# Filling the slots table in five parts from SP, spreading the first modulation by a product, and k's sum as a column of kv

## The chip, the cores and the metric
The kernel is one program on one core of a Trainium2 chip. The metric is the device time in microseconds of one execution, the median of several runs. Five engines work side by side: TensorE (PE; its weight loads are shown apart as PEld), VectorE (DVE), ScalarE (ACT), GpSimd (POOL) and SyncE (SP, which here mostly issues DMAs). They meet only through semaphores.

## The reference
Two transformer layers on x of shape (4, 1024, 128), each with an adaptive-norm modulation computed from a vector c per batch. Cut to what matters here, which is layer 0:

```
mod = (silu(L0_c) @ L0_wmod).reshape(4, 6, 1, -1)      # sa, ca, ga, sb, cb, gb
ga  = (2 * (ga >= 0) - 1) * maximum(abs(ga), 0.25)     # gb likewise
h = layernorm(x) * (1 + ca) + sa
# linear attention, 16 heads of 8, inside L0_attn_ref(h)
q = elu(q) + 1 ; k = elu(k) + 1
kv   = einsum('bhnd,bhne->bhde', k, v)
ksum = sum(k over n)
z    = 1 / (einsum('bhnd,bhd->bhn', q, ksum) + 1e-6)
attn_out = einsum('bhnd,bhde->bhne', q, kv) * z
# projection, residual, layer norm, MLP; x = x + ga * that
# then h = layernorm(x) * (1 + cb) + sb; x = x + gb * mixture(h), top 4 of 16 experts and 2 shared
```

Layer 1 has softmax attention with 16 heads of 64 and a position bias, and a mixture of 8 experts, top 2, with a shared part. Its routed tokens are sorted through a table in DRAM: for every expert there is a region of 4096 rows, and each token row is scattered to its slot.

## The kernel before
The residual x (four batches of 1024 tokens) stays in SBUF as `xs`. The program has five stages: a setup; a loop over the four batches that does all of layer 0 and the first norm of layer 1 (stored to DRAM as `hkeep`); layer 1's attention, a software pipeline over 64 heads, by far the longest; a loop over batches that routes tokens and scatters rows into `slots`; and a loop over 72 tiles of 128 rows of `slots` for the experts.

Each engine has its own instruction stream, in program order. At the end of a stage or a batch every engine calls `end_batch` (drain, count up `batch_ended`, wait for `batch_open`), and SP calls `meet`: it waits until all four others have ended, clears the batch's semaphores and opens the next. So a batch starts when the last of the five is there.

**Setup.** SP issues the loads (lines 327 to 346), waits for the modulation rows computed by PE and VectorE (`mod_one`), stores them to DRAM (`modrows`, line 349), waits until they have landed, and loads them back spread over 128 partitions: `modnext` (line 331: the first two rows, for the batch to come), and for every batch `modwo` and `modd` (lines 356, 357: eight DMAs). Before the first meeting it waits for `next_mod` and `rows_in`. VectorE computes the moments of batch 0's x, finishes the modulation rows (752 to 765), copies constants (768 to 777, `set_done`), treats the transposed modulations (782 to 793), then normalizes batch 0's x (`first_norm`, line 742), applies modnext (line 800), takes the moments again and normalizes a second time. POOL fills constants and one SBUF tile, `spair`, with the mark EMPTY, and raises to the power -0.5 (line 517). ScalarE waits for `set_done` and `pool_set` and writes EMPTY over the whole `slots` table from `spair` with two DMAs (lines 1232, 1233), then goes to the meeting. `filled` counts them; POOL waits for it before layer 1's attention and VectorE in each batch ahead of the first norm of layer 1.

**A layer-0 batch.** PE turns the normalized x (line 1455), projects k and v per tile (1490) and q (1493). VectorE and ScalarE apply elu + 1 to k (817, 820) and to q (822, 824), and VectorE copies v. PE then makes k's column sum (eight products with a column of ones, line 1497), kv (eight products summed in one bank, 1500), the denominators (eight products with 16 columns, 1505) and the numerators (eight products with 128 columns, 1509). VectorE masks ksum by head (828) and kv (830), adds the projection's bias to h (831), adds eps to all denominators at once (834), inverts them (836) and multiplies each half of the numerators by them (841). PE turns the result (1513), VectorE and ScalarE copy a half each (844, 1242), PE projects (1517), and VectorE adds the residual (647). The MLP, the experts and layer 1's first norm follow. In each batch SP issues the whole modulation rows `modb` (line 375) and `modnext` for the next batch, and towards the end stores `hkeep` (381). After the loop SP issues the attention's first eight loads (388 to 399) and then `hT` (408), for which it waits.

## Time and profile before
| | us |
|---|---|
| median of 3 runs (2627.24 to 2631.41) | 2630.47 |
| the profiled execution | 2632.31 |
| its span, first to last instruction | 2630.30 |
| PE, DVE, ACT, POOL busy | 2311.4, 1772.2, 1280.1, 1394.8 |
| setup, until PE's first transposes of batch 0 | 65.4 |
| layer-0 batches 0 and 1 | 122.3 and 119.2 |

PE is busy for 88% of the span, nearly all of it in layer 1's attention. Such a share says little about a stage: the setup and the layer-0 batches are a chain of short steps that pass from engine to engine, so each is read from its timeline and its chain of waits. The granted TensorE clock, 1.00 for 2.4 GHz and 0.50 for 1.2 GHz, was 0.916 on average. DMA moved 83.5 MB in all.

### The profile page before, as it was taken

To read this page: it belongs to the slowest core of one execution; us is meant where nothing else is said; L and a number is where in the kernel's file an instruction comes from. 1 tells how busy PE (TensorE), PEld (TensorE's weight loads), DVE (VectorE), ACT (ScalarE), POOL (GpSimd) and SP (SyncE) were. 2 spreads that over 40 slices of the span, in tenths; PEclk is the share of its full clock that TensorE was granted. 3 is DMA by queue.
4 is the path that set the end of the run, shared out by engine and by line. 5 is a ranking of instruction groups with operands and counts; after the bars stand their busy time and mean duration, and the time that the engine had idled before them with its cause. 6 is when DMAs were issued, how large, how long until landed. Compare 5 with 4: busy or idle time off the path is not lost.

```text
span 2630.3 us, 40209 instructions
## 1 busy us (share of the span) xinstructions
PE 2311.4 (88%) x10587; PEld 1388.2 (53%) x10608; DVE 1772.2 (67%) x4580; ACT 1280.1 (49%) x1705; POOL 1394.8 (53%) x757
## 2 busy tenths in 40 slices
PE   1778786949999999999999999999999976649995
PEld 0645554625555655555555555555555543326664
DVE  3475656557777777877877877877877754544444
ACT  0222121326666666666666666666666641114442
POOL 1120111107777777777777777777677764542321
PEclk6788787859999999999999999999999987869998
DMA  9200000000000000000000000000000011001114
GB/s 357 85 23 0 22 0 22 0 27 14 9 14 13 11 20 13 11 13 12 12 20 12 13 11 12 14 18 12 14 10 11 14 52 75 26 25 45 42 42 121
DMA packets 68566, 83.45 MB, mean 32 GB/s; under 512 B 17732, under 2 KB 55236, under 8 KB 68360
## 3 DMA queue, kind: packets, MB, share of 16 engines
q1 hardware_dynamic: 59784, 56.57, 7.0%
q10 hardware_dynamic: 4384, 17.37, 1.9%
q0 software_dynamic: 4352, 8.99, 1.1%
q8 instruction: 18, 0.29, 0.0%
q14 instruction: 28, 0.23, 0.0%
HBM read 52.33 MB, written 32.66 MB: 32 GB/s over the span
## 4 chain that ended last, share of the span: by engine, by line
PE 81%; DVE 7%; issue 4%; POOL 3%; ACTq 2%; ACT 1%; DMA 1%; SPq 1%; POOLq 0%; DVEq 0%
PE P L1655 17%; PE P L1619 11%; PE P L1640 9%; PE P L1641 9%; PE P L1606 4%; PE P L1828 2%; PE P L1832 2%; PE P L1851 2%; POOL slots L598 2%; PE P L1662 2%; PE P L1673 2%; PE P L1588 2%; PE P L1541 2%; PE P L1555 2%; PE P L1455 2%
## 5 line engine op out<-in xcount | busy, mean ns | idle before, releaser
L1305 ACT ACTIVATE big<-P 128x1024 f32<-128x1024 f32 x512 | 511.9, 1021 | 188.3 <-PE P L1641 84.4
L937 DVE CUSTOM_DVE_ANT_0 big<-P,near 128x512 f32<-128x512 f32 x512 | 348.8, 681 | 231.5 <-PE P L1619 231.2
L1655 PE MATMUL P<-big,V 128*64 128x512 f32 x2048 | 481.4, 602 | 0.0
L560 POOL TENSOR_TENSOR spair<-spair,big 128x1024 f32<-128x1024 f32 x192 | 457.3, 2382 | 13.2
L560 POOL TENSOR_TENSOR opair<-opair,big 128x1024 f32<-128x1024 f32 x192 | 456.9, 2380 | 13.8 <-ACT big L1305 0.7
L1619 PE MATMUL P<-Ka,Qa 96*128 96x512 f32 x1024 | 452.2, 463 | 4.8 <-DVE mhalf L937 3.3
L1640 PE MATMUL P<-Qa,Ka 97*128 97x512 f32 x1024 | 407.8, 398 | 0.5 <-ACT big L1305 0.5
L940 DVE TENSOR_REDUCE mhalf<-P 128x1 f32<-128x512 f32 x512 | 349.2, 682 | 85.9 <-PE P L1619 75.9
L1641 PE MATMUL P<-Qb,Kb 128*128 128x512 f32 x1024 | 406.5, 397 | 0.0
L1619 PEld LDWEIGHTS P<-Ka,Qa 96*128 96x128 f32 x1024 | 186.0, 191 | 224.3 <-issue 118.6
L547 POOL TENSOR_TENSOR big<-big,sinv 128x512 f32<-128x512 f32 x64 | 81.8, 1278 | 377.6 <-DVE sinv L912 377.6
L1655 PEld LDWEIGHTS P<-big,V 128*64 128x64 f32 x2048 | 130.1, 136 | 262.8 <-issue 207.4
L912 DVE RECIPROCAL sinv<-sinv 128x128 f32<-128x128 f32 x256 | 240.9, 943 | 14.7 <-ACT sinv L1291 12.7
L1640 PEld LDWEIGHTS P<-Qa,Ka 97*128 97x128 f32 x1024 | 195.0, 190 | 50.0 <-issue 14.9
L1641 PEld LDWEIGHTS P<-Qb,Kb 128*128 128x128 f32 x1024 | 195.5, 191 | 45.5
L531 POOL TENSOR_TENSOR rstd<-veps,halfneg 128x4 f32<-128x4 f32 x40 | 41.1, 1027 | 240.5 <-DVE veps L635 240.5
L617 POOL DMA_INDIRECT yrows<-xn,tidx x72 | 69.1, 960 | 176.6 <-DVE xn L1189 176.6
L1455 PE MATMUL P<-identf,xn 128*128 128x128 f32 x128 | 36.9, 432 | 136.9 <-DVE xn L641 77.1
L950 DVE TENSOR_TENSOR P<-P,near 128x128 f32<-128x128 f32 x512 | 149.6, 292 | 8.1 <-PE P L1641 6.1
L1606 PE MATMUL P<-hT,wqk 128*128 128x512 f32 x256 | 135.0, 609 | 16.7 <-SPq L410 10.1
L1275 ACT ACTIVATE Qa<-P 64x512 fp32r<-64x512 f32 x128 | 75.7, 591 | 132.7 <-PE P L1641 101.4
L1295 ACT ACTIVATE Qa<-P 1x1024 fp32r<-1x1024 f32 x64 | 64.8, 1012 | 144.7 <-PE P L1624 144.7
(273 smaller groups left out, 3585.8 us busy)
## 6 DMA issues: line engine op xcount, KB each, us to landing
slots<-spair ACTq DMA_DIRECT2D x1, 16896.0 KB, 56.9
Ka<-auxrows SPq DMA_DIRECT2D x66, 128.0 KB, 2.2
big<-in_wex SPq DMA_DIRECT2D x8, 768.0 KB, 9.1
xt<-slots SPq DMA_DIRECT2D x76, 66.0 KB, 1.8
wqk<-in_whead SPq DMA_DIRECT2D x66, 64.0 KB, 1.8
near<-in_aux SPq DMA_DIRECT2D x66, 64.0 KB, 1.8
big<-yrows SPq DMA_DIRECT2D x8, 512.0 KB, 7.2
modb<-modrows SPq DMA_DIRECT2D x4, 768.0 KB, 4.3
```

The costliest lines, as they stand in the source:

```text
L560: pool.tensor_tensor(psum8[s][:, :], psum8[s][:, :], pfull[:, j % RING, :], ALU.add).then_inc(S["p_added"], 1)
L912: dve.reciprocal(sinv[s][:, cols], sinv[s][:, cols]).then_inc(S["s_inv"], 1)
L937: dve.tensor_tensor_reduce(scratch, P[:, 6 + i, :], near[s][:, left:left + HALF], -1.0, 3.0e38, ALU.add, ALU.min, mhalf[:, i, t:t + 1]).th ...
L940: dve.tensor_reduce(mhalf[:, i, t:t + 1], P[:, 6 + i, :], AX.X, ALU.max, negate=True).then_inc(S["max_red"], 1)
L950: dve.tensor_tensor(block, block, near[s][:, ZERO:ZERO + 128], ALU.add).then_inc(S["biased"], 1)
L1305: act.activation(pfull[:, j, :], banks(2 * (j % 2)), ACT.Exp, scale=DH1 ** -0.5).then_inc(S["exp_done"], 1)
L1455: tr = pe.transpose(bank_t(bank, t), src[:, t, :], identf[:, :])
L1606: pe.matmul(P[:, 5, :], wqk[s][:, :], half(hT, i), start=True, stop=True).then_inc(S["qk_mm"], 1)
L1619: pe.matmul(P[:, 6 + i, :], tile(Qa[s][0:MROW, :], t), half(Ka[s][0:MROW, :], i), start=True, stop=True).then_inc(S["max_mm"], 1)
L1640: pe.matmul(P[:, bank + i, :], tile(Ka[s][0:KEXACT, :], j), half(Qa[s][0:KEXACT, :], i), start=True, stop=False)
L1641: mm = pe.matmul(P[:, bank + i, :], tile(Kb[s], j), half(Qb[s], i), start=False, stop=True)
L1655: mm = pe.matmul(P[64 * i:64 * i + 64, 4, :], V1[:, j, s, :], half(pfull[:, j, :], i), start=(j == 0), stop=(j == T - 1))
```

## The change
The `slots` table is no longer filled by ScalarE in the setup. SP issues it in five parts: one in each layer-0 batch (128 partitions x 11 pieces of 768 words, behind the batch's modulation loads) and a tail (128 x 4 pieces of 33 words) ahead of the attention's loads. The source is `later`, which POOL fills instead of `spair`; POOL alone waits for all five, at the end of layer 1's attention.

The first modulation of batch 0 is not loaded from DRAM: PE multiplies a row of ones with the two rows of batch 0 that it needs and so puts them on all 128 partitions of a PSUM bank, and VectorE reads them there. The first load of `modnext` and the waits for it go. In VectorE's setup order the first norm, its modulation and the moments stand ahead of the constants and the transposed modulations.

In the attention of layer 0, v has a column of ones beside its 128 columns (written by POOL in each batch), so kv's product has k's sum as its 129th column. Masked kv and masked ksum lie side by side, and one product of 144 columns per tile gives numerators and denominators. VectorE adds eps, inverts and multiplies once per half. The sum's and the denominators' own products go. Leading blanks are cut below.

```diff
-       "kv_mm", "ks_mm", "kv_masked", "ks_masked", "num_mm", "den_mm", "den_eps", "den_inv", "o0_tok", "o0_turned", "o0_done", "o0_done_a",
+       "kv_mm", "kv_masked", "ks_masked", "num_mm", "v0_ones", "den_eps", "den_inv", "o0_tok", "o0_turned", "o0_done", "o0_done_a",
...
-  "mod_one", "mod_out", "modT_copied", "set_done", "pool_set", "batch_ended", "batch_open", "x_in", "h_kept", "rows_in", "we_in", "passed", "filled", "scattered",
+  "mod_one", "mod_spread", "mod_out", "modT_copied", "set_done", "pool_set", "batch_ended", "batch_open", "x_in", "h_kept", "rows_in", "we_in", "passed", "filled", "scattered",
...
+onerow = sb("onerow", [1, 128])
...
-small = opair[:, 0:256].rearrange("p (a b) -> p a b", b=128)
+kvs = opair[:, 0:D + H0]
...
+v0x = A[:, 4:6, :].rearrange("p a b -> p (a b)")[:, 0:T * (D + 1)].rearrange("p (t c) -> p t c", c=D + 1)
+o0 = A[:, 2, :]
+onum = P[:, 0:4, :].rearrange("p a (t c) -> p (a t) c", c=2 * D)
...
+empty = later[:, :, :].rearrange("p k e -> p (k e)")
+blank = slots.rearrange("(p q) c -> p (q c)", p=128)
+chunk = NBLK * E1
+quarter = blank.shape[1] // (B * chunk)
+rest = blank.shape[1] - B * quarter * chunk
+assert 0 < rest <= 4 * chunk and rest % 4 == 0
+NFILL = B + 1
...
-NSET, NPOOL = 2, 11
+NSET, NPOOL = 2, 12
...
-load_mods(0)
...
-sp.wait_ge(S["next_mod"], 16)
...
+    part = blank[:, bass.ds(b * (quarter * chunk), quarter * chunk)].rearrange("p (a c) -> p a c", c=chunk)
+    sp.dma_start(part, over(empty, [128, quarter, chunk])).then_inc(G["filled"], 16)
...
+tail = blank[:, B * quarter * chunk:].rearrange("p (a c) -> p a c", a=4)
+sp.dma_start(tail, over(empty[:, 0:rest // 4], [128, 4, rest // 4])).then_inc(G["filled"], 16)
...
+pool.memset(onerow[:, :], 1.0).then_inc(G["pool_set"], 1)
...
-pool.memset(spair[:, :].bitcast(I32), EMPTY).then_inc(G["pool_set"], 1)
+pool.memset(later[:, :, :].rearrange("p k e -> p (k e)").bitcast(I32), EMPTY).then_inc(G["pool_set"], 1)
...
+    pool.memset(v0x[:, :, D:D + 1], 1.0).then_inc(S["v0_ones"], 1)
...
-pool.wait_ge(G["filled"], 32)
...
+pool.wait_ge(G["filled"], 16 * NFILL)
...
-dve.tensor_tensor(gs, tmp, sg, ALU.mult)
+dve.tensor_tensor(gs, tmp, sg, ALU.mult).then_inc(G["mod_sgn"], 1)
...
+dve.wait_ge(G["mod_sgn"], 3)
+first_norm(h, x0, 1, "f_h")
+dve.wait_ge(G["mod_spread"], 1)
+for step, (m, op) in enumerate(((1, ALU.mult), (0, ALU.add))):
+    dve.wait_ge(S["f_h"], T + step)
+    dve.tensor_tensor(h[:, :, :], h[:, :, :], over(P[:, 4, m * D:(m + 1) * D], tens), op).then_inc(S["f_h"], 1)
+dve.wait_ge(S["f_h"], T + 2)
+first_moments(h, 2)
...
-first_norm(h, x0, 1, "f_h")
-dve.wait_ge(S["next_mod"], 16)
-for step, (m, op) in enumerate(((1, ALU.mult), (0, ALU.add))):
-    dve.wait_ge(S["f_h"], T + step)
-    dve.tensor_tensor(h[:, :, :], h[:, :, :], over(modnext[:, m, :], tens), op).then_inc(S["f_h"], 1)
-dve.wait_ge(S["f_h"], T + 2)
-first_moments(h, 2)
...
-    dve.tensor_copy(tok(A[:, 4, :]), kpsum[:, :, D:2 * D]).then_inc(S["v0_copied"], 1)
+    dve.tensor_copy(v0x[:, :, 0:D], kpsum[:, :, D:2 * D]).then_inc(S["v0_copied"], 1)
...
-    dve.wait_ge(S["ks_mm"], 1)
...
-    dve.tensor_scalar(small[:, 1, 0:H0], by_head, P[:, 7, 0:1], None, ALU.mult).then_inc(S["ks_masked"], 1)
...
-    dve.tensor_tensor(small[:, 0, :], P[:, 6, 0:D], mask[:, :], ALU.mult).then_inc(S["kv_masked"], 1)
+    dve.tensor_scalar(kvs[:, D:D + H0], by_head, P[:, 6, D:D + 1], None, ALU.mult).then_inc(S["ks_masked"], 1)
+    dve.tensor_tensor(kvs[:, 0:D], P[:, 6, 0:D], mask[:, :], ALU.mult).then_inc(S["kv_masked"], 1)
...
-    dve.wait_ge(S["den_mm"], 1)
-    dve.tensor_scalar(A[:, 1, 0:T * H0], P[:, 2, 0:T * H0], EPS_ATTN, None, ALU.add).then_inc(S["den_eps"], 1)
-    dve.wait_ge(S["den_eps"], 1)
-    dve.reciprocal(A[:, 3, 0:T * H0], A[:, 1, 0:T * H0]).then_inc(S["den_inv"], 1)
-    dve.wait_ge(S["den_inv"], 1)
...
+        ts, hs = slice(i * TPH, (i + 1) * TPH), slice(i * TPH * H0, (i + 1) * TPH * H0)
...
-        z = A[:, 3, i * TPH * H0:(i + 1) * TPH * H0].unsqueeze(2).to_broadcast([128, TPH * H0, DH0])
-        dve.tensor_tensor(half(A[:, 5, :], i).rearrange("p (h e) -> p h e", e=DH0),
-                          P[:, i, :].rearrange("p (h e) -> p h e", e=DH0), z, ALU.mult).then_inc(S["o0_tok"], 1)
+        dve.tensor_scalar(A[:, 1, hs].rearrange("p (t h) -> p t h", h=H0), onum[:, ts, D:D + H0], EPS_ATTN, None, ALU.add).then_inc(S["den_eps"], 1)
+        dve.wait_ge(S["den_eps"], i + 1)
+        dve.reciprocal(A[:, 3, hs], A[:, 1, hs]).then_inc(S["den_inv"], 1)
+        dve.wait_ge(S["den_inv"], i + 1)
+        z = A[:, 3, hs].rearrange("p (t h) -> p t h", h=H0).unsqueeze(3).to_broadcast([128, TPH, H0, DH0])
+        dve.tensor_tensor(half(o0, i).rearrange("p (t h e) -> p t h e", h=H0, e=DH0),
+                          onum[:, ts, 0:D].rearrange("p t (h e) -> p t h e", e=DH0), z, ALU.mult).then_inc(S["o0_tok"], 1)
...
-    dve.wait_ge(G["filled"], 32)
...
-blank = slots.rearrange("(p q) c -> p (q c)", p=128)
-whole = blank.shape[1] // N
-act.dma_start(blank[:, 0:whole * N].rearrange("p (a b) -> p a b", b=N), over(spair[:, :], [128, whole, N])).then_inc(G["filled"], 16)
-act.dma_start(blank[:, whole * N:], spair[:, 0:blank.shape[1] - whole * N]).then_inc(G["filled"], 16)
...
+pe.wait_ge(G["mod_one"], 1)
+pe.wait_ge(G["pool_set"], NPOOL)
+first_rows = A[0:1, 6:8, :].rearrange("p a b -> p (a b)")[:, 0:2 * D]
+pe.matmul(P[:, 4, 0:2 * D], onerow[:, :], first_rows, start=True, stop=True).then_inc(G["mod_spread"], 1)
...
-pe.wait_ge(G["mod_one"], 1)
...
+    pe.wait_ge(S["v0_ones"], 1)
...
-        mm = pe.matmul(P[:, 7, 0:1], tile(A[:, 2, :], t), onecol[:, :], start=(t == 0), stop=(t == T - 1))
-    mm.then_inc(S["ks_mm"], 1)
-    for t in range(T):
-        mm = pe.matmul(P[:, 6, 0:D], tile(A[:, 2, :], t), tile(A[:, 4, :], t), start=(t == 0), stop=(t == T - 1))
+        mm = pe.matmul(P[:, 6, 0:D + 1], tile(A[:, 2, :], t), v0x[:, t, :], start=(t == 0), stop=(t == T - 1))
...
-    for t in range(T):
-        mm = pe.matmul(P[:, 2, t * H0:(t + 1) * H0], tile(A[:, 0, :], t), small[:, 1, 0:H0], start=True, stop=True)
-    mm.then_inc(S["den_mm"], 1)
...
-        pe.matmul(bank_t(0, t), tile(A[:, 0, :], t), small[:, 0, :], start=True, stop=True).then_inc(S["num_mm"], 1)
+        pe.matmul(onum[:, t, 0:D + H0], tile(A[:, 0, :], t), kvs, start=True, stop=True).then_inc(S["num_mm"], 1)
...
-            tr = pe.transpose(bank_t(6, t), tile(A[:, 5, :], t), identf[:, :])
+            tr = pe.transpose(bank_t(6, t), tile(o0, t), identf[:, :])
```

## Rows read from the trace of the kernel before

**Rows 1.** Chain of waits, 0 to 420 us. Columns: start us, us, what.
```profile
25.72 38.71 ACTq L1233
65.45 1.96 PE P L1455 x8
...
187.75 1.96 PE P L1455 x8
...
306.91 1.96 PE P L1455 x8
```

**Rows 2.** Page, DMA issues: out<-in engine op xcount, KB each, us to landing.
```profile
slots<-spair ACTq DMA_DIRECT2D x1, 16896.0 KB, 56.9
```

**Rows 3.** Timeline, 0 to 75 us: start us, us, engine, line, op, tiles, xcount, [idle before].
```profile
15.75 0.41 DVE L765 TENSOR_SCALAR big<-big 4x512 f32<-4x512 f32 x1
...
22.03 2.14 DVE L742 TENSOR_SCALAR hp<-xs,mv,rstd 128x128 f32<-128x128 f32 x8
...
28.83 0.36 SPq L331 DMA_DIRECT2D modnext<-modrows  x1
29.23 1.23 SPq L356 DMA_DIRECT2D modwo<-modrows  x1
...
36.68 2.48 DVE L800 TENSOR_TENSOR hp<-hp,modnext 128x1024 f32<-128x1024 f32 x2 [12.51 <-DMA modnext<-modrows]
...
37.79 0.66 SPq L357 DMA_DIRECT2D modd<-modrows  x1
...
41.81 1.64 POOL L517 TENSOR_TENSOR rstd<-veps,halfneg 128x8 f32<-128x8 f32 x1 [30.25 <-DVE veps L737]
43.49 2.14 DVE L742 TENSOR_SCALAR xn<-hp,mv,rstd 128x128 f32<-128x128 f32 x8 [1.76 <-POOL rstd L517]
```

**Rows 4.** Waits of SP's queue, 0 to 66 us: total us, times, longest.
```profile
SPq L371 <- DMA modd<-modrows: 14.2, 1, 14.2
```

**Rows 5.** Timeline of batch 1, 182 to 218.5 us.
```profile
200.10 1.23 DVE L820 SCALAR_TENSOR_TENSOR big<-P,big 128x1024 f32<-128x1024 f32 x1
...
201.48 2.21 PE L1497 MATMUL P<-onecol,big 128*128 128x1 f32 x16 [2.04 <-DVE big L820]
...
203.55 3.37 PE L1500 MATMUL P<-big 128*128 128x128 f32 x16
203.59 1.22 DVE L824 SCALAR_TENSOR_TENSOR big<-P,big 128x1024 f32<-128x1024 f32 x1 [1.12 <-ACT big L1240]
...
208.46 2.03 PE L1509 MATMUL P<-opair,big 128*128 128x128 f32 x16
...
209.96 1.29 DVE L841 TENSOR_TENSOR big<-P,big 128x512 f32<-128x512 f32 x2
...
213.41 0.69 DVE L647 TENSOR_TENSOR big<-P,hp 128x512 f32<-128x512 f32 x1 [1.32 <-PE P L1517]
```

**Rows 6.** Timeline of batch 0, 65 to 102 us.
```profile
77.52 1.22 DVE L820 SCALAR_TENSOR_TENSOR big<-P,big 128x1024 f32<-128x1024 f32 x1
...
88.05 3.76 PE L1509 MATMUL P<-opair,big 128*128 128x128 f32 x16
...
94.83 0.69 DVE L647 TENSOR_TENSOR big<-P,hp 128x512 f32<-128x512 f32 x1 [1.44 <-PE P L1517]
```

**Rows 7.** Windows: us, busy of PE, PEld, DVE, ACT, POOL; granted clock, DMA share, GB/s.
```profile
88.00:92.00 4.00, 4.00 (x19) 4.00 (x20) 2.09 (x4) 0.00 (x0) 0.00 (x0) 0.50 0.00 0
...
208.00:210.00 2.00, 2.00 (x20) 2.00 (x20) 1.66 (x4) 0.00 (x0) 0.00 (x0) 1.00 0.00 0
```

**Rows 8.** DMA queues, 25 to 29 us: packets, MB, share of 16 engines.
```profile
q10 hardware_dynamic: 103, 0.42, 26.6%
```

**Rows 9.** Chain of waits, 536 to 600 us.
```profile
549.05 3.93 DMA hT<-hkeep
```

**Rows 10.** Groups by form, 60 to 560 us: count, busy us, mean ns, idle before.
```profile
L836 DVE RECIPROCAL big<-big 128x128 f32<-128x128 f32 x4 | 3.8, 954 | 0.1
...
L664 DVE RECIPROCAL rmax<-rmax 128x8 f32<-128x8 f32 x4 | 0.8, 203 | 0.1
```

## The prediction
> **What bounds the kernel now.** I read the chain of waits first. The stage that the change touches ahead of the first batch ends on one entry: ScalarE's queue, held for 38.71 us from 25.72 us on by its second DMA into the slots table (line 1233), and then PE's first transposes of the batch loop at 65.45 [rows 1]. The DMA issued just ahead of it moves 16.9 MB and takes 56.9 us to land [rows 2]; the second could be issued only as the first drained, and ScalarE cannot join the meeting of the engines (end_batch) while its queue is held. The timeline says what else was due: VectorE ends its setup work at 43.49 + 2.14 = 45.6, and SP, whose last row load is issued at 37.79 + 0.66 [rows 3], then waits 14.2 us for it [rows 4], until 52.7. So 64.4 is ScalarE's own, 52.7 SP's, 45.6 VectorE's. The rest of the span (attention of layer 1, experts) keeps its instructions and is left at its own time. Inside a layer-0 batch I read the timeline of batch 1: from the end of k's last VectorE step (200.10 + 1.23 = 201.33) to the residual after the projection (213.41) are 12.08 us [rows 5]; in batch 0 the same stretch, 78.75 to 94.83, is 16.08 us [rows 6], because there TensorE stood at the granted clock 0.50 (1.2 GHz) where batch 1 had 1.00 (2.4 GHz) [rows 7].
>
> **Setup, part by part.** Removed: both DMAs of ScalarE and their hold. ScalarE then waits only for set_done. What is late next, in turn:
>
> VectorE's new order. The last modulation step ends at 16.16 [rows 3]. Then come the first normalization (2.14), the two modulating steps (2.48, now with an operand in PSUM; the 1024-element VectorE step of line 824, which reads PSUM, takes 1.22 [rows 5], so no difference) and the moments (39.16 to 41.81 before, 2.6): 16.2 + 2.1 + 2.5 + 2.6 = 23.4. The constants and the transposed modulations took from there to 22.03, 5.9 us: 29.3. They also cover POOL's root, 1.64 us, which VectorE stood waiting for before. The second normalization, 2.14: 31.4. Before, the two modulating steps stood waiting until 36.68 for modnext's load through DRAM; that wait goes. In its place stands one TensorE product of 256 columns, ready to start when the modulations are (16.2), while VectorE still normalizes until 18.4. The nearest row, eight products of 128 columns in 3.76 us at the low clock [rows 6], makes 0.5 us for 128 columns and 1 us for 256: covered, with 1 us to spare.
>
> SP. The modulation rows are stored, and SP sees them landed at 28.8, when it issues modnext's load [rows 3]. In 25 to 29 us the fill's queue took 26.6% of the DMA time [rows 8], so without it the backlog ends about 1 us sooner: 27.8. modnext's own load is dropped. Eight row loads follow. Each issue cost 1.23 us with the fill in flight, yet the one before them, same kind, 0.36 [rows 3]. Both ends: 8 x 0.4 = 3.2 or 8 x 1.2 = 9.6. I take 3.2, because ScalarE's held second DMA is what is special to the slow ones. The last issue ends at 31.0; landing: 512 KB of hT take 3.93 [rows 9], which bounds 128 KB from above; I take 2.2: 33.0. With the slow issues, 39.3. The meeting and the start of the loop: before, 64.43 to 65.45, 1.0; after SP's own wait 0.8. So PE starts at 33.8 (slow issues: 40.1) instead of 65.45: **31.6 us** gained (25.4). VectorE's 31.4 is hidden below SP's 33.0.
>
> POOL: one memset of a row more, one of 768 columns for one of 1024; done before 6 us, nobody waits. In each batch a memset of eight columns stands ahead of POOL's wait for modb; POOL would be idle there: 0.
>
> A rule of the Trainium skill speaks against this gain (DMA: Bandwidth & Descriptors, "Issuing engines are not separate DMA queues"): issuing from another engine only saves the sequencer's issue time, "usually small". By it, moving the fill would bring under 1 us. The trace differs on size: here the issue time of one DMA is 38.71 us. The rule does hold for the bytes, which stay the same.
>
> **The fill, where it goes.** Each batch gets 128 x 11 pieces of 3 KB, 4.3 MB, behind modb and modnext in SP's queue. At the pace of before (16.9 MB in 56.9 us, beside others) that is up to 14.6 us a batch. Queued behind it on SP is the store of hkeep, some 120 us later in the batch; the modulation tiles are issued ahead of it. I cost it at 0. Cover: in batch 0 of before the old fill was under way for some 15 us more (25.3 + 56.9 = 82.2) [rows 2], and line 820 started 12.07 us after the first transposes (65.45 to 77.52) [rows 1, 6]; batch 1, without a fill, took 12.35 (187.75 to 200.10) [rows 1, 5]. If that cover is gone, each part costs up to 14.6 us.
> The tail, 512 pieces of 132 bytes, comes ahead of the nine loads that open the attention, of which the last, hT, is waited for (3.93 us) [rows 9]. One issue more, 0.4 us, and packets that run under the eight issues between: I take **0.6 us** lost, ends 0 and 2.5.
> The Trainium skill (same page, Specifications) says that pieces under 512 bytes are read, modified and written; no row of before has such stores, and the sum goes by the ends just given.
>
> **Layer-0 attention.** Counted from the end of line 820 (t = 0). Before, in batch 1: k's column products at 0.15 for 2.21, kv at 2.22 for 3.37, the denominators' products, the numerators at 7.13 for 2.03, and VectorE's two divisions at 8.63 for 1.29, with eps and the reciprocal done beside the numerators [rows 5]. From the second division's end (9.92) to the residual, 2.16.
> After: kv (129 columns) starts at 0.15. At the high clock its 16 passes take 2.0 (numerators' row, 2.03), at the low clock 3.4. But q's chain ends at 203.59 + 1.22 = 3.48 whatever PE does [rows 5], and both maskings (16 and 128 columns) follow it: a division of 512 columns takes 0.65 [rows 5], so I put them at 0.6 together. The numerators start at 4.1 (4.4 with kv slow) and have 144 columns of 128: 2.03 x 9/8 = 2.3 at the high clock, 3.76 x 9/8 = 4.2 at the low one; first half complete at 5.4 or 6.4. Now eps, reciprocal and division stand on the path once per half. A reciprocal of 128 columns is 0.954, of 8 it is 0.203 [rows 10], so 64 take 0.203 + 56 x 0.0063 = 0.55; eps, as small a step, 0.25; the division 0.65; with gaps 1.55. Two halves: high clock 5.4 + 3.1 = 8.5, residual at 10.6; low clock: second half complete at 8.3, divided at 9.9, residual at 12.3 with slower transposes. The bias addition (1024 columns, so 1.22, after the maskings, until 5.3) just fits in front of the first half. Against 12.08 a batch gains 1.5 or loses 0.2. TensorE now has a gap of about 2 us between kv and the numerators, which batch 1 of before did not have, so I count on both clocks: 0.9 a batch. Batch 0 took 122.3 in all (65.45 to 187.75), batch 1 119.2 (187.75 to 306.91, the next batch's first transposes) [rows 1]: batch 0 ran its stretch at the low clock, which a fresh start need not repeat. 4 x 0.9 + 3.1 = **6.7 us** (ends 0 and 10).
> The Trainium skill (TensorE: Matmul & The Clock Gate, Part 1) holds that the default state is throttled and "activity releases the throttle". By that rule the products taken out were also what held the clock up, and the change could end at the low-clock value; this is rival 2.
>
> **Sum.** 31.6 + 6.7 - 0.6 = 37.7. The profiled execution is 2632.31 with a span of 2630.30, 1.8 above the median of the three runs; 2632.3 - 37.7 = 2594.6 in that execution, and from the median 2630.47, **2592.8**.
>
> **The rivals.**
> 1. Slow row issues stay: something else than the fill (the number of broadcast rows queued, say) makes each 1.2 us. For it: no row shows eight of them behind each other without a fill. Against: modnext's 0.36 in the same busy queues. Gain 25.4 + 6.1 = 31.5: **2599**. 0.2.
> 2. The clock: numerators, transposes and projection at 1.2 GHz in each batch. For: the new gap; against: in batch 1 the low clock lasted only over kv. Each batch -0.2, batch 0 gains as its stretch falls from 16.1 to 12.3, 3.8, partly given back: 31.6 + 3 - 0.6 = 34: **2596.5**. 0.15.
> 3. Slower: a part of the fill holds its batch. Mechanism: while 4.3 MB are on the 16 DMA engines, an engine's code or the modb load comes late, and the batch waits for the part's end. Place: the first 15 us of each batch; price up to 14.6 each, 58.4 in all, against 37.7: **2651**. It decides the sign from 9.4 us a part on. Against: the 12.07 beside the 12.35 us above. 0.02.
> 4. It does not do what it says: something behind ScalarE, such as the row loads landing at 52.7 as before, sets the meeting, so that the gain is 65.4 - 53.7 = 11.7 + 6.1: **2613**. Against: those loads shared the engines with the fill. 0.05.
>
> **How the numbers follow.** Forecast 0.58, rivals as given. The forecast's own ends: row landing +-1.5, attention 0 to 10, tail 0 to 2.5: 2588 to 2600. The range takes in rivals 1 and 2 and a little of the attention's best case: 2586 to 2602. What a measurement of this kernel can tell from no change is about 0.2%, 5 us. Faster by more than that holds the forecast and rivals 1, 2 and 4: 0.97; slower 0.02; same 0.01.
>
> **What would show it.** Right: PE's first transposes at 33 to 35 us; row issues of 0.4 us; no ScalarE hold; the last wait of setup SP's, on modd; the fill's queue time inside each batch with unchanged starts of line 820's step; from that step's end to the residual 10.6 (high clock) to 12.3 us. Wrong: a first start past 38 us (rival 1 or 4), batches over 120 us (rival 3), or the opening of attention later by more than 2 us after hkeep's store.

## The result

The changed kernel takes **2588.39 us** (median of 4 runs, 2586.66 to 2590.54) against 2630.94 for the kernel before in the same comparison: ratio 0.984, 95% interval 0.9823 to 0.9857, so 42.5 us less. The forecast was 2592.8 with the range 2586 to 2602. The profiled execution took 2586.66 us with a span of 2584.8 (before: 2632.31 and 2630.3), at a mean granted clock of 0.927 (before 0.916).

| part | forecast us | measured us | where it is read |
|---|---|---|---|
| start of the batch loop | 31.6 | 27.95 | first transposes 65.45 -> 37.50 |
| the four batches | 6.7 | 13.4 | 478.82 -> 465.41, start of batch 0 to the last store of hkeep |
| opening of the attention | -0.6 | -1.1 | last store of hkeep to its first projection 8.93 -> 10.07 |
| the rest | 0 | 5.2 in the profiled pair, 2.3 between the medians | spans, less the lines above |

The total is near because two misses partly cancel: setup came out 3.7 below the forecast, the batches 6.7 above it. That part is luck. Both are explained below. A batch is counted here from VectorE's first step in it (37.44 and 65.40 for batch 0), some 0.05 us ahead of PE's first transposes.

**Setup after.** The timeline from 12 us to the first batch (start us, us, engine, line, operation; in brackets the idle time before and what ended it). It answers to [rows 3].

```profile
15.97 1.22 PE L1457 MATMUL P<-big,onerow 1*128 1x256 f32 x2 [1.96 <-DVE big L780]
18.07 2.48 DVE L787 TENSOR_TENSOR hp<-hp,P 128x1024 f32<-128x1024 f32 x2
...
28.54 2.14 DVE L757 TENSOR_SCALAR xn<-hp,mv,rstd 128x128 f32<-128x128 f32 x8
29.44 0.35 SPq L366 DMA_DIRECT2D modwo<-modrows  x1
...
32.68 0.43 SPq L367 DMA_DIRECT2D modd<-modrows  x1
...
37.50 1.94 PE L1467 MATMUL P<-identf,xn 128*128 128x128 f32 x8 [20.31 <-SPq L373]
```

The first modulation is spread by PE in 1.22 us at 15.97, and the modulating steps follow the first normalization without a wait (before: at 36.68, with 12.51 us idle [rows 3]). VectorE ends at 30.7. SP sees the modulation rows landed at 29.4 and issues the first of the eight row loads in 0.35 us and the others in 0.43 each (before some 1.2). The waits of SP's queue (waited for: us in total, times, longest) answer to [rows 4]:

```profile
SPq L380 <- DMA modd<-modrows: 3.5, 1, 3.5
```

The last wait is SP's on modd, 3.5 us instead of 14.2, and ScalarE's queue no longer shows. The page's DMA issues (KB each, us to landing) give the fill's four parts, and modb, which is issued ahead of each part. [rows 2] had one DMA of 16896 KB and 56.9 us:

```profile
slots<-later SPq DMA_DIRECT2D x4, 4224.0 KB, 15.4
...
modb<-modrows SPq DMA_DIRECT2D x4, 768.0 KB, 5.1
```

**The batches after.** The chain of waits (start us, us, what) has the first transposes of three batches; it answers to [rows 1].

```profile
37.50 1.95 PE P L1467 x8
...
156.04 1.96 PE P L1467 x8
...
272.22 1.95 PE P L1467 x8
```

The batches take 118.57, 116.20, 116.04 and 114.60 us; before, 122.34, 119.11, 119.39 and 117.98. Now the attention of batch 1 in the timeline, which answers to [rows 5]:

```profile
168.44 1.22 DVE L835 SCALAR_TENSOR_TENSOR big<-P,big 128x1024 f32<-128x1024 f32 x1
...
169.77 2.02 PE L1510 MATMUL P<-big 128*128 128x129 f32 x16 [1.99 <-issue]
...
171.92 1.22 DVE L839 SCALAR_TENSOR_TENSOR big<-P,big 128x1024 f32<-128x1024 f32 x1 [1.12 <-ACT big L1249]
...
173.63 2.20 PE L1516 MATMUL P<-opair,big 128*128 128x144 f32 x16 [1.84 <-DVE opair L844]
174.89 0.23 DVE L850 TENSOR_SCALAR big<-P 128x64 f32<-128x64 f32 x1 [0.27 <-PE P L1516]
...
179.78 0.69 DVE L662 TENSOR_TENSOR big<-P,hp 128x512 f32<-128x512 f32 x1 [1.32 <-PE P L1524]
```

From the end of k's last step (168.44 + 1.22 = 169.66) to the residual at 179.78 are 10.12 us (before 12.08). kv stands at 2.02 us, not 3.37, and is done at 171.79, before q's last step even starts (171.92). The numerators start 3.97 after k's step, take 2.20, and eps, reciprocal and division of the first half begin 1.26 after them. In batch 0 the same products ran at the lower clock level, which answers to [rows 6]. Its kv took longer too:

```profile
50.77 2.77 PE L1510 MATMUL P<-big 128*128 128x129 f32 x16 [1.99 <-issue]
...
54.63 4.18 PE L1516 MATMUL P<-opair,big 128*128 128x144 f32 x16 [1.10 <-DVE opair L844]
...
62.30 0.69 DVE L662 TENSOR_TENSOR big<-P,hp 128x512 f32<-128x512 f32 x1 [1.32 <-PE P L1524]
```

There the stretch is 11.64 us (before 16.08): the numerators cost 4.18 and the first half's eps waits until 56.93. The granted clock fell to 0.50 at 51.9, 1.1 us into kv and before PE's wait behind it, and was back at 1.00 from 58.7 on.

**The clock.** Windows in batch 1 (us, busy of PE, PEld, DVE, ACT, POOL; granted clock, DMA share, GB/s): first before, then after, each time first over kv and then at 35.5 us into the batch, within the first MLP product. They answer to [rows 7].

```profile
203.00:206.00 3.00, 3.00 (x15) 3.00 (x15) 1.37 (x2) 0.55 (x1) 0.00 (x0) 0.50 0.00 0
...
223.30:227.00 3.70, 3.70 (x6) 1.44 (x5) 1.18 (x1) 1.38 (x2) 0.00 (x0) 0.52 0.00 0
```

```profile
170.00:172.00 2.00, 1.79 (x16) 1.60 (x15) 0.88 (x2) 1.06 (x1) 0.00 (x0) 1.00 0.76 287
...
191.50:195.20 3.70, 3.70 (x9) 1.21 (x7) 0.00 (x0) 2.65 (x4) 0.00 (x0) 0.96 0.00 0
```

Before, the clock was at 0.50 (1.2 GHz) from 203.0 us on, while the eight one-column products of k's sum (x16 in the trace, 201.48 to 203.69) still ran, and kv ran at 0.50 behind them. After, kv stands at 1.00, with a part of the fill on the DMA engines at share 0.76. And 35.5 us into the batch, before is still at 0.52 where after has 0.96. The two windows lie at different places of the product, because after begins it 1.9 us earlier in the batch: counted from the product's own start, the clock is back at 1.00 after 5.3 us in the kernel before and after 3.9 us in the changed one. The product takes 9.46 us instead of 10.10.

### The profile page after: what moved, and what is told of

Read it like the earlier page. It is cut to its first block, busy times and chain, and to the rows that moved or that the text cites. A ratio compares the mean times of both kernels' runs of the same rounds, so it can differ in the third digit from the quotient of the medians.

```text
span 2584.8 us, 39973 instructions
## 1 busy us (share of the span) xinstructions
PE 2287.3 (88%) x10461; PEld 1364.4 (53%) x10482; DVE 1772.1 (69%) x4588; ACT 1280.0 (50%) x1705; POOL 1391.5 (54%) x762
## 4 chain that ended last, share of the span: by engine, by line
PE 81%; DVE 7%; issue 4%; POOL 3%; ACT 2%; DMA 2%; SPq 1%; POOLq 0%; DVEq 0%; ACTq 0%
PE P L1662 18%; PE P L1626 11%; PE P L1647 9%; PE P L1648 9%; PE P L1613 4%; PE P L1835 2%; PE P L1839 2%; PE P L1858 2%; PE P L1669 2%; POOL slots L613 2%; PE P L1680 2%; PE P L1595 2%; PE P L1548 2%; PE P L1467 2%; PE P L1562 2%
## 5 line engine op out<-in xcount | busy, mean ns | idle before, releaser
L1662 PE MATMUL P<-big,V 128*64 128x512 f32 x2048 | 481.3, 602 | 0.0
L1467 PE MATMUL P<-identf,xn 128*128 128x128 f32 x128 | 37.5, 438 | 103.1 <-DVE xn L656 74.6
```

The source lines that it names most:

```text
L1467: tr = pe.transpose(bank_t(bank, t), src[:, t, :], identf[:, :])
L1662: mm = pe.matmul(P[64 * i:64 * i + 64, 4, :], V1[:, j, s, :], half(pfull[:, j, :], i), start=(j == 0), stop=(j == T - 1))
```

## The experiments

Ratios are to the kernel before on the same chip; "first transposes" is the start of batch 0. "Stretch" is the time from the end of k's last VectorE step to the residual.

**1. The setup half alone** (everything of the change but the attention). Against the changed kernel:

```diff
-kvs = opair[:, 0:D + H0]
+small = opair[:, 0:256].rearrange("p (a b) -> p a b", b=128)
...
-        mm = pe.matmul(P[:, 6, 0:D + 1], tile(A[:, 2, :], t), v0x[:, t, :], start=(t == 0), stop=(t == T - 1))
+        mm = pe.matmul(P[:, 7, 0:1], tile(A[:, 2, :], t), onecol[:, :], start=(t == 0), stop=(t == T - 1))
+    mm.then_inc(S["ks_mm"], 1)
+    for t in range(T):
+        mm = pe.matmul(P[:, 6, 0:D], tile(A[:, 2, :], t), tile(A[:, 4, :], t), start=(t == 0), stop=(t == T - 1))
```

> Only the setup half of the change: the fill in five parts from SP, the first modulation spread by a product. Layer-0 attention as before. Theory (the halves add up): PE's first transposes at 37.5 us as in the changed kernel instead of 65.4, so 28.0 us gained; the batches keep their lengths (about 122 for the first, 119 for the others); the opening of the attention costs 1.1 us. Time about 2604. Rival (the halves interact): the earlier start alone changes where TensorE's clock rises and falls in the batches, and part of the 13.4 us that the four batches became shorter comes from the start; then batches are 1 us or more shorter each and the time is 2601 or less.

Measured: 2601.08 us, 0.9881 (0.9862 to 0.99). First transposes at 36.9 (37.5 in the changed kernel). The batches add up to 481.7, in which both of the first two have the long stretch, 16.22 and 16.08. The first profile of before had that in batch 0 alone and 478.8 in all; the second profile of before (experiment 12) has 481.3 and 16.08 in batch 1. So, within what two profiles of one kernel differ by, the setup half changes nothing in the batches that the kernel before doesn't also show from one execution to the next, and the fill's parts, present here, cost them nothing.

**2. The attention half alone** (setup and fill as before). Against the kernel before it is experiment 1's diff the other way round:

```diff
-        mm = pe.matmul(P[:, 7, 0:1], tile(A[:, 2, :], t), onecol[:, :], start=(t == 0), stop=(t == T - 1))
...
+        mm = pe.matmul(P[:, 6, 0:D + 1], tile(A[:, 2, :], t), v0x[:, t, :], start=(t == 0), stop=(t == T - 1))
```

> Only the layer-0 attention half of the change; setup and fill as before. First transposes stay at 65.4 us. Theory (the halves add up): the stretch from the end of k's last VectorE step to the residual falls from 16.1 (batch 0) and 12.1 (others) to 11.6 and 10.1, and the batches are 13.4 us shorter in sum: about 2617.5. Rival (the halves interact): only the 10.3 us of the stretch are its own, the other 3.1 go with the clock elsewhere and may not come: about 2620.5.

Measured: 2618.17, 0.9948 (0.9931 to 0.9966). Batches 117.76, 116.03, 116.00 and 114.57, in all 14.5 less than before, the stretch 10.13 in each. The batch loop starts at 68.9, 3.5 later than in the profile of before: ScalarE is held for 41.46 us here. The halves give 29.6 and 12.5, together 42.1 of the 42.5. The gain in the batches is the attention's alone, and twice what I forecast. No batch of this profile has the numerators at 4.18 us.

**3. The changed kernel with the fill on ScalarE again**, all else as changed.

```diff
-    sp.dma_start(part, over(empty, [128, quarter, chunk])).then_inc(G["filled"], 16)
...
+act.dma_start(blank[:, 0:whole * N].rearrange("p (a b) -> p a b", b=N), over(spair[:, :], [128, whole, N])).then_inc(G["filled"], 16)
+act.dma_start(blank[:, whole * N:], spair[:, 0:blank.shape[1] - whole * N]).then_inc(G["filled"], 16)
```

> The changed kernel with the fill put back on ScalarE in the setup, as before (two DMAs, source a tile filled by POOL, waits as before); the spread product, VectorE's new order and the new attention stay. Theory (ScalarE's held queue sets the setup): first transposes at 65.4 us again, the eight row issues of SP at 1.2 us each again, the fill's queue share in batch 0 again, and the opening of the attention 1.1 us shorter: 2588.4 + 28 - 1 = about 2615.5. Rival (the spread product and the order bring part of the 28 us): first transposes well below 65 us.

Measured: 2617.28, 0.9944 (0.9926 to 0.9962). Its timeline:

```profile
27.25 36.38 ACTq L1236 DMA_DIRECT2D slots<-spair  x1
...
29.10 0.35 SPq L359 DMA_DIRECT2D modwo<-modrows  x1
29.49 1.22 SPq L360 DMA_DIRECT2D modd<-modrows  x1
...
64.66 1.94 PE L1461 MATMUL P<-identf,xn 128*128 128x128 f32 x8 [48.18 <-SPq L366]
```

ScalarE is held for 36.38 us and the first transposes are at 64.66. Moving the fill is worth 27 us of setup; with the fill where it was, all the rest of the change brings the setup 0.8. The row issues are back at 1.2 us, but for the first of them: it is the fill that makes them slow, not their number. Rival 1 falls. But the hold of ScalarE's queue, which my forecast named as the cause, does not do it by itself, and neither does the fill's landing. In experiment 2, where ScalarE is held until 67.9, SP's last row load is quick again long before:

```profile
39.82 0.44 SPq L360 DMA_DIRECT2D modd<-modrows  x1
```

And modb is issued in 0.35 us at 65.38 in the kernel before, while the fill still lands (until about 82). The slow issues lie in the first 13 us or so behind the fill's issue. What ends them was not tested.

**4. The changed kernel with the first modulation loaded through DRAM, in the old order.**

```diff
+load_mods(0)
...
+sp.wait_ge(S["next_mod"], 16)
...
-dve.wait_ge(G["mod_sgn"], 3)
-first_norm(h, x0, 1, "f_h")
-dve.wait_ge(G["mod_spread"], 1)
...
+first_norm(h, x0, 1, "f_h")
+dve.wait_ge(S["next_mod"], 16)
...
-pe.matmul(P[:, 4, 0:2 * D], onerow[:, :], first_rows, start=True, stop=True).then_inc(G["mod_spread"], 1)
```

> The changed kernel with the first modulation loaded through DRAM and VectorE's old order, the fill still in parts from SP. Theory (both matter once the fill is gone): modnext lands at about 33 us, and VectorE then still has 2.5 + 2.6 + 1.6 + 2.1 = 8.8 us to do, so it ends at 42 and the first transposes are at 43 instead of 37.5: about 2594. Rival (SP's row loads hide it): VectorE is done by 37, only the one issue more shows, 0.5 us: about 2589.

Measured: 2593.27, 0.9858 (0.984 to 0.9876), 4.9 above the changed kernel, and the first transposes at 42.13, 4.6 later. VectorE's last normalization starts at 39.11 there (28.54 when the product spreads the row). So this half of the setup counts, though ScalarE's hold had hidden it: VectorE would have been the next bound. The run takes back the load and the order together and doesn't say what each is worth.

**5. SP's rows out of the way.** The changed kernel with the eight row loads and the tail issued behind the load of hT, and POOL waiting for the rows ahead of layer 1's attention.

```diff
-for b in range(B):
-    sp.dma_start(modwo[:, b, :], rows_of[b, MODS + 2].partition_broadcast(128)).then_inc(G["rows_in"], 16)
-    sp.dma_start(modd[:, b, :, :], rows_of[b, MODS + 3:MODS + 5].partition_broadcast(128)).then_inc(G["rows_in"], 16)
...
-sp.wait_ge(G["rows_in"], 32 * B)
...
-sp.dma_start(tail, over(empty[:, 0:rest // 4], [128, 4, rest // 4])).then_inc(G["filled"], 16)
...
 sp.dma_start(hT[:, :], hkeep[0]).then_inc(S["hT_in"], 16)
+for b in range(B):
+    sp.dma_start(modwo[:, b, :], rows_of[b, MODS + 2].partition_broadcast(128)).then_inc(G["rows_in"], 16)
+    sp.dma_start(modd[:, b, :, :], rows_of[b, MODS + 3:MODS + 5].partition_broadcast(128)).then_inc(G["rows_in"], 16)
+sp.dma_start(tail, over(empty[:, 0:rest // 4], [128, 4, rest // 4])).then_inc(G["filled"], 16)
...
+pool.wait_ge(G["rows_in"], 32 * B)
```

> The changed kernel with SP's eight row loads (modwo, modd) and the fill's tail issued behind the attention's load of hT, and POOL waiting for the rows ahead of the attention; the first meeting no longer waits for them. Theory (SP's row loads set the setup at 36.6 us, VectorE is next at 30.7): first transposes at about 31.5 instead of 37.5, 6 us less; the opening of the attention 0.7 to 1.1 us shorter; about 2581.5, give or take 3 for the clock in the batches. Rival (something else stands behind the row loads, such as the load of modb through the same queue or the store's landing at 29.3): first transposes at 33 or later, 2584 to 2586.

Measured: 2583.22, 0.9813 (0.9799 to 0.9826), 5.2 less than the changed kernel. First transposes:

```profile
27.68 2.14 DVE L757 TENSOR_SCALAR xn<-hp,mv,rstd 128x128 f32<-128x128 f32 x8
...
30.71 1.94 PE L1467 MATMUL P<-identf,xn 128*128 128x128 f32 x8 [14.90 <-SPq L369]
```

They start 0.9 after VectorE's last step (29.82), 6.8 earlier than with the rows. So in the changed kernel SP's rows were the bound and VectorE's chain the next, as the forecast had it (it wrote 33.0 and 31.4; the trace says 36.6 and 30.7). The opening of the attention is 9.75, hardly better than 10.07. hT is issued as early behind hkeep's store as before the change (4.85 us) and lands 4.1 later, at 506.4, but SP issues the rows and the tail before it asks for hT: its last issue ends at 507.04, and PE starts at 507.24.

**6. The fill in one piece on SP**, between the meeting and the loop.

```diff
+whole = blank[:, 0:B * quarter * chunk].rearrange("p (a c) -> p a c", c=chunk)
+sp.dma_start(whole, over(empty, [128, B * quarter, chunk])).then_inc(G["filled"], 16)
...
-    sp.dma_start(part, over(empty, [128, quarter, chunk])).then_inc(G["filled"], 16)
```

> The changed kernel with the fill's four parts as one DMA of 16.9 MB, issued by SP between the first meeting and the loop. Theory (only ScalarE's hold ahead of the meeting cost time; the bytes hide): modb and modnext of batch 0 are queued behind it and land some 50 us into the batch. The scaled second MLP weights need modb at about 46 us into the batch, so batch 0 is up to 15 us longer; the other batches keep their lengths. About 2600. Rival (the queue serves them side by side): batch 0 keeps its 118.6 us, 2588. In the routing loop of layer 1 the executions with the fill on ScalarE were some 4 us longer than those with parts on SP; if the one large DMA is what does it, this run has the longer ones, and if ScalarE's queue is, it has the shorter ones.

Measured: 2621.15, 0.9955 (0.994 to 0.997). Batch 0 takes 149.0 us, 30.4 more than with parts, the others 116.3, 116.1 and 114.6. Its waits from 30 to 180 us:

```profile
POOL big L535 <- DMA modb<-modrows: 54.3, 1, 54.3
```

POOL, which folds the modulation into the MLP's weights, waits 54.3 us for modb. SP's timeline shows why:

```profile
38.08 36.66 SPq L386 DMA_DIRECT2D modb<-modrows  x1
```

The load that comes behind the 16.9 MB on the same queue holds SP for 36.66 us, as the fill's second DMA had held ScalarE for 38.71: the hold has moved with the fill, and does not belong to ScalarE. Only then does the load get onto the queue, and it lands 17 us later still. I had priced this at 15 us at most. Cutting the fill into parts and issuing each behind the modb load of its own batch makes the move free: this is rival 3's mechanism, present as soon as the bytes stand ahead of modb. Which of the two it needs, the smaller parts or the order, was not tried apart.

**7. The products of k's sum put back**, ahead of kv, into a bank that nobody reads; the rest of the change stays.

```diff
     pe.wait_ge(S["v0_ones"], 1)
+    for t in range(T):
+        pe.matmul(P[:, 7, 0:1], tile(A[:, 2, :], t), onecol[:, :], start=(t == 0), stop=(t == T - 1))
     for t in range(T):
```

> The changed kernel with k's eight column-sum products back ahead of kv (into a free bank, their result unused; the sum still comes as a column of kv). Theory (the clock): they are 2.0 us of work that does not hold TensorE's clock up; in most batches kv then runs at 1.2 GHz for 3.4 us where it ran for 2.1 at 2.4 GHz, the numerators start at 6.2 us behind k's last VectorE step instead of 3.97, and the residual stands at about 12.4 instead of 10.1: four batches lose about 9 us, 2597. Rival (work alone): the numerators start at 4.9, since q's chain hides most of the 2 us; residual at 11.0; four batches lose 3.6 us, 2592.

Measured: 2603.81, 0.9889 (0.9874 to 0.9904). Batch 1 in its timeline:

```profile
170.44 1.22 DVE L835 SCALAR_TENSOR_TENSOR big<-P,big 128x1024 f32<-128x1024 f32 x1
...
171.77 2.10 PE L1510 MATMUL P<-onecol,big 128*128 128x1 f32 x16 [1.99 <-issue]
...
173.73 3.48 PE L1512 MATMUL P<-big 128*128 128x129 f32 x16
...
177.26 0.24 DVE L843 TENSOR_SCALAR opair<-mask,P 128x16 f32<-128x16 f32 x1 [2.12 <-PE P L1512]
...
177.84 2.20 PE L1518 MATMUL P<-opair,big 128*128 128x144 f32 x16 [0.62 <-DVE opair L844]
...
183.99 0.69 DVE L662 TENSOR_TENSOR big<-P,hp 128x512 f32<-128x512 f32 x1 [1.32 <-PE P L1526]
```

The unused products take 2.10, and kv behind them 3.48 instead of 2.02. The masking, which waited for q's step before, now waits for kv (2.12 us idle ahead of 177.26), and the stretch is 12.33. The batches are 121.56, 119.28, 119.40 and 118.00, 478.2 in all, within 1 us each of before (122.34, 119.11, 119.39, 117.98). So 12.8 of the 13.4 us hang on these eight products a batch: their own time, the low clock over kv that goes with them, and what is lost later in the batch. The stretch in batches 1 to 3, 12.33, is even 0.25 longer than before (12.08), so the one product of 144 columns and the division by halves bring nothing there by themselves. What the run doesn't tell apart is the kind of product and the 2 us by which it puts kv off, for no busier set of the same length was tried. And the one-column products are not needed for the fall: in the changed kernel the clock falls during kv in one batch of four, in the next experiment in all four.

**8. One eps and one reciprocal** for all tiles, behind the last numerator.

```diff
+dve.wait_ge(S["num_mm"], T)
+dve.tensor_scalar(A[:, 1, 0:T * H0].rearrange("p (t h) -> p t h", h=H0), onum[:, :, D:D + H0], EPS_ATTN, None, ALU.add).then_inc(S["den_eps"], 1)
+dve.wait_ge(S["den_eps"], 1)
+dve.reciprocal(A[:, 3, 0:T * H0], A[:, 1, 0:T * H0]).then_inc(S["den_inv"], 1)
...
-    dve.wait_ge(S["num_mm"], (i + 1) * TPH)
-    dve.tensor_scalar(A[:, 1, hs].rearrange("p (t h) -> p t h", h=H0), onum[:, ts, D:D + H0], EPS_ATTN, None, ALU.add).then_inc(S["den_eps"], 1)
...
-    dve.reciprocal(A[:, 3, hs], A[:, 1, hs]).then_inc(S["den_inv"], 1)
```

> The changed kernel with eps and the reciprocal once over all eight tiles, behind the last numerator, instead of once per half. Theory (the per-half order hides one half's steps behind the second half's products): 0.29 + 0.95 then stand behind the last product, the first division starts about 3.97 + 2.3 + 1.3 = 7.6 us behind k's last VectorE step and the residual is at 11.1 instead of 10.1: 4 us more in sum. Rival (two halves pay the fixed cost of a step twice and hide little): 10.1 to 10.4, up to 1 us in sum.

Measured: 2599.48, 0.9873 (0.9858 to 0.9888), 11 more than the changed kernel where 4 were expected; the stretch 13.86, 13.87, 13.84 and 13.82. Batch 1:

```profile
168.88 2.53 PE L1510 MATMUL P<-big 128*128 128x129 f32 x16 [1.99 <-issue]
...
172.75 4.18 PE L1516 MATMUL P<-opair,big 128*128 128x144 f32 x16 [1.33 <-DVE opair L844]
176.97 0.29 DVE L848 TENSOR_SCALAR big<-P 128x128 f32<-128x128 f32 x1 [3.23 <-PE P L1516]
...
182.65 0.69 DVE L662 TENSOR_TENSOR big<-P,hp 128x512 f32<-128x512 f32 x1 [2.23 <-PE P L1524]
```

The numerators take 4.18 in all four batches. From their end to the residual are 5.72 us (182.65 - 176.93) against 3.95 in the changed kernel (179.78 - 175.83): 1.8 us. About half of that is the order of the steps, which puts nothing of eps, reciprocal and division beside the numerators; the other half is the clock, which falls again at 180.5, ahead of the projection (3.67 us instead of 2.05). The next experiment has a batch whose projection runs at the high clock, and there the same way takes 4.81, 0.9 more than 3.95. The remaining 2 us are the clock over the numerators, which I had not expected: nothing ahead of them was changed. It is lost before PE's wait. In each of the four batches kv itself takes 2.46 to 2.80 us instead of 2.02, and in batch 1 the clock falls at 170.2, 1.4 us into kv. The next experiment asks whether work in the wait brings it back.

**9. The same, with the gap filled.** Experiment 8 with six products of zeros (bf16, 512 columns, into a free bank) in TensorE's wait between kv and the numerators.

```diff
+def idle(n):
+    for _ in range(n):
+        pe.matmul(P[:, 7, :], zerob[:, 0:128], zerob[:, :], start=True, stop=True)
...
     mm.then_inc(S["kv_mm"], 1)
+    idle(6)
```

> The kernel of one eps and one reciprocal (2599.48 us, numerators 4.18 us in all four batches, 13.84 from the end of k's last VectorE step to the residual), with six zero products of 512 columns in TensorE's wait between kv and the numerators. If the low clock over the numerators comes from that wait (theory), they take 2.2 us in all four batches, the residual stands at 11.9 and the time is about 8 us less, 2591. If it comes from something earlier in the batch (rival), the numerators stay at 4.18 in most batches and the time stays near 2599.

Measured: 2597.35 in one run, beside 2628.36 of before. The numerators take 2.1 to 2.2 in all four batches, and the stretch is 11.85, 12.09, 12.03 and 12.00. Batch 0 is the one that compares like with like, since there the clock falls during kv in both. First experiment 8, then this one:

```profile
49.71 2.80 PE L1510 MATMUL P<-big 128*128 128x129 f32 x16 [1.99 <-issue]
```

```profile
50.90 2.76 PE L1514 MATMUL P<-big 128*128 128x129 f32 x16 [2.00 <-issue]
...
55.72 2.12 PE L1521 MATMUL P<-opair,big 128*128 128x144 f32 x16
```

With the zeros in the wait the clock is back at 1.00 from 55.4 on, just ahead of the numerators (2.12 us); without them it stays at 0.50 over all of them (4.17 us from 53.58 on). In batches 1 to 3 of this run kv already stands at 2.02: the clock had not fallen when the zeros began, so these batches don't show what the zeros do. Why the fall has moved there is open. So the wait is not where the clock is lost, as the expectation had it; work in it ends the low stretch sooner, in the one batch that can show it. The time does not follow it: the batches are 118.44, 119.31, 119.40 and 117.99, against 118.95, 119.33, 119.41 and 117.99 in experiment 8. The timelines of batch 1 show where the 1.8 us of batch 1 went, first experiment 8, then this one:

```profile
190.80 9.32 PE L1530 MATMUL P<-hT,wfc 128*128 128x512 f32 x16 [1.02 <-ACT hT L1239]
```

```profile
189.96 10.16 PE L1535 MATMUL P<-hT,wfc 128*128 128x512 f32 x16 [1.02 <-ACT hT L1239]
```

The MLP's first product starts 35.4 and 34.0 us into the batch, 1.5 earlier, and takes 0.8 us longer; the rest is gone by the batch's end. In experiment 8 the clock is low from 180.5 to 183.9 and from 187.3 to 194.1, in this one from 178.3 to 181.7 and from 185.1 to 195.4. What the numerators gained, the later steps pay back. A stretch alone is not the price of the clock.

**10. PE kept busy in three places.** Experiment 5 with the same products of zeros in three of PE's waits in a batch: five behind the first transposes, six behind kv, twelve behind the projection.

```diff
+                if n:
+                    idle(n)
                 pe.wait_ge(S["hT_dve"], TR_TAGS[tag] + 1)
...
-                turn("a1", 0)
+                turn("a1", 0, n=5)
...
                 mm.then_inc(S["kv_mm"], 1)
+                idle(6)
...
+                idle(12)
```

> The kernel with the late row loads (a8_rowslate) and products of zeros into a free bank where TensorE waits in a layer-0 batch: 5 after the first transposes, 6 between kv and the numerators, 12 after the projection (512 columns each, about 0.21 us at 2.4 GHz, 0.43 at 1.2). Theory (the clock in the waits is what splits the batches): the numerators take 2.2 us in all four batches, the residual stands at 10.1 in all four, the k and v projection and the first MLP products run at 2.4 GHz for more of their time, and the batches are 114 us or shorter where a8 had 116.4 to 118.8: 10 us less in sum, 2573. Rival (idle products cost more than they bring): at the low clock they overrun their waits by 1 to 2 us each and the rises come no earlier; batches of 117 us or more, 2585 or more.

Measured: **2576.73**, 0.9788 (0.9772 to 0.9804), 6.5 less than without them and the fastest version here. First the projection of k and v in experiment 5's batch 0, then this kernel's, and kv of its batch 3:

```profile
34.95 6.04 PE L1502 MATMUL P<-wqkv,hT 128*128 128x256 f32 x16 [2.30 <-ACT hT L1239]
```

```profile
33.64 2.04 PE L1502 MATMUL P<-zerob 128*128 128x512 bf16 x5
...
36.15 3.69 PE L1508 MATMUL P<-wqkv,hT 128*128 128x256 f32 x16 [0.47 <-ACT hT L1239]
...
386.76 3.66 PE L1516 MATMUL P<-big 128*128 128x129 f32 x16 [2.00 <-issue]
```

The projection starts 4.24 behind the first transposes in both (30.71 to 34.95, 31.91 to 36.15), so the zeros cost nothing there, and takes 3.69 instead of 6.04. While the zeros run the clock is low (0.65 on average from 33.5 to 36.0), over the projection it is at 1.00. The batches add up to 457.4 against 466.8, 9.4 less; between the medians 6.5 remain (the loop starts 1.2 later here, and two batches of the routing loop fell into the slow pattern of the last section, one in experiment 5). The fill runs beside both projections, so it is the clock and not the transfers that makes the projection slow, here and in each batch of the changed kernel (5.77 us in batch 1).

The gain is uneven. The batches take 111.9, 114.9, 115.8 and 114.8 us, in experiment 5 116.9, 118.8, 116.5 and 114.6: 5.0, 3.8, 0.7 and nothing. In batches 0 and 1 it stays; batch 1 was the long one of experiment 5. In batches 2 and 3 the projection is shorter as well (4.16 and 4.29 for 5.95 and 5.75), but the MLP's first product takes 10.35 and 9.92 where it had 9.49 and 9.46, as in experiment 9, and in batch 3 the clock falls as kv begins, in spite of the zeros (3.66 us, the last line above), so that its stretch is 10.98. The expectation of 114 us or less in every batch holds in one. What each of the three places brings was not tried apart.

**11. The changed kernel, once more.**

> The changed kernel once more, unchanged, for a second profile. If a batch is long or short by chance of the execution (theory), another batch than batch 0, or none or two, has its numerators at 4.18 us and a length near 118.7, and the sum of the four stays within 3 us of 465.4; if it belongs to batch 0 (rival, since its start differs), batch 0 is again the long one.

Measured: 2589.91 in one run. The batches are 116.42, 118.71, 116.41 and 114.67, 466.2 in all (465.4 in the first profile). The numerators take 4.18 in batch 1 and 2.1 to 2.2 in the others; in the first profile that was batch 0. Again kv of the long batch is at 2.54 and the others' at 2.02. So which batch is long differs from one execution to the next, and it doesn't belong to batch 0.

**12. The kernel before, once more**, for the rest of the difference.

> The kernel before, profiled once more. In the routing loop of layer 1 its first profile had slow scatter issues (about 1.65 us instead of 0.96) in all four batches, the changed kernel in one. Theory (chance of how the scatters fall beside VectorE's steps on the tile map): another profile of the same kernel can show another number of such batches, and its routing loop is shorter by 1.2 us for each one fewer. Rival (the way of the fill decides): four again.

Measured: 2631.58 in one run. The batches are 121.75, 122.40, 119.23 and 117.96 (stretches 14.81, 16.08, 12.08 and 12.07), 481.3 in all. Against the second profile of the changed kernel the batches differ by 15.1 us, against 13.4 in the first pair, so the attention's gain is known to some 2 us only. From the start of the routing loop to the end it takes 463.7 us, where the first profile of the same kernel had 467.4.

## Why the prediction came out as it did

**The bound of the setup: right.** ScalarE's held queue set the start (experiment 3 brings 64.7 back), and what was late next was SP, then VectorE (experiment 5), in the order forecast. The forecast of 0.4 us an issue came true, but the reason that it gave, ScalarE's held second DMA, is not borne out (experiment 3).

**The size of SP's step: 3.7 short.** The terms were: rows landed 27.8, issues 3.2, landing 2.2, meeting 0.8. Measured: 29.4, 3.7, 3.5 and 0.9, and 0.2 more had been lost in adding up. The first was the wrong step: I took from [rows 8] that without the fill's 26.6% the backlog would end a us sooner. It ended 0.6 later (29.4 for 28.8). The issues cost 0.43 each with 0.04 between them, as the low end said. The landing was taken at 2.2 from a bound of 3.93 for a DMA four times as large; eight loads of broadcast rows in a row behave like the bound, not like the size.

**Rival 1 (1.2 us an issue): refuted**, by the timeline after and by experiment 3.

**The fill at no cost inside the batches: right**, within the 2 us or so by which profiles of one kernel differ. Each part stands behind modb and is small; experiment 6 takes both away and pays 30 us, twice the price that I had put on a part. What I had not seen is that the hold itself would come along.

**The tail: 1.1 for 0.6.** hT's load is issued 5.50 us behind hkeep's store instead of 4.83: of these 0.67, the tail's own issue is 0.39, and the loads behind it are issued a little slower. The other 0.46 is landing: hT took 4.39 (before 3.93 [rows 9]), beside these:

```profile
hT<-hkeep SPq DMA_DIRECT2D x1, 512.0 KB, 4.4
...
slots<-later SPq DMA_DIRECT2D x1, 66.0 KB, 3.9
```

**The attention's path at the high clock: right.** 10.12 us for a forecast of 10.6; the numerators start at 3.97 for 4.1 and take 2.20 for 2.3. q's chain, not kv, is what they wait for.

**The clock: the step that failed.** I wrote that PE's new gap of 2 us between kv and the numerators would put the batches partly at the low clock, and took 0.9 a batch between 1.5 and -0.2 (the middle would have been 0.65). The gap is there (1.84 us idle ahead of 173.63), and the numerators run at 1.00 behind it in three batches of four. Where they don't, the clock had fallen during kv, before the gap. What I didn't weigh is the other side of the same ledger: the products of k's sum that were taken out stood directly ahead of the dip over kv in my own rows (2.21 us, then 3.37 [rows 5]), and with them the dip went in three batches of four and came back in all four when they were put back (experiment 7). The clock's return in the MLP also came sooner, and this brought some 0.9 to 1.4 us in batches 1 to 3, a term that my sum didn't have at all. In us from batch 0 to 3, the batches gained 3.8, 2.9, 3.4 and 3.4; the stretch alone 4.4, 2.0, 2.0 and 2.0. Why the changed kernel keeps the clock up over kv in three batches and experiment 8 in none stays open.

**Rival 2 (low clock over the numerators): it happens, in one batch of four**, and in all four of experiment 8. Its reason, the new gap, is not what the traces show: the clock falls ahead of it, during kv, and the gap only falls into the low stretch. By the rival a stretch would be 12.3; it is 11.64, because the clock is back at 1.00 from 58.7 on, ahead of most of the transposes and of the projection, which the rival had counted as slow. The sentence on the Trainium skill (TensorE: Matmul & The Clock Gate, Part 1: activity releases the throttle) expected the products taken out to have held the clock up. The runs do not bear this out for one-column products (experiment 7), and agree for wide ones in batch 0 of experiments 9 and 10.

**Rivals 3 and 4** did not come: no batch is over 120 us, and the rows landed at 36.6, not 52.7.

**The rest.** Between the medians it is 2.3 us, below what a measurement can tell. In the profiled pair it is 5.2, of which 3.7 is the chance of the profile of before (experiment 12), as the last section shows.

## What to carry to other kernels

When a held queue is taken off the path, price the next two engines by the landing of their last DMA as the trace shows it for the same kind of load, not scaled by bytes. Moving a large background fill to another engine moves the hold with it: here it was free behind the loads that a batch waits for and in parts that land within the batch, and cost 30 us in one piece ahead of them. Products of one column in front of a wide set were worth more than their own time here. Where PE waits anyway, wide products of zeros can bring the high clock back for what follows; whether the gain stays must be read over the whole stage and in every batch, since a low stretch put off in one place can come back in the next.
